# Norm, projection and dense attention put into one block each, the softmax maxima turned in f32 into four strips, and one division per unit

## The reference

```
h = layernorm(x) * (1 + ca) + sa
x = x + ga * L0_attn(h)        # 16 heads of 8, elu + 1 features, rotary, softmax over all 1024 keys, plus a 3-tap conv
x = x + gb * L0_ffn(h)         # two windowed-attention layers
x = x + ga * L1_attn(h)        # 16 heads of 8, softmax over all 1024 keys, then the mask of j >= i
x = x + gb * L1_ffn(h)         # four rounds of a four-expert mixture
```

## Time and profile before

| | |
|---|---|
| median of 3 runs | 1806.47 us (1805.66 to 1809.19) |
| the profiled execution | 1807.94 us |
| its span, first to last instruction | 1805.8 us |
| mean granted TensorE clock | 0.927 |
| busy share of the span | PE 87%, DVE 77%, ACT 66%, POOL 35% |
| first dense attention, first score to last value product | about 108 to 442 us |
| second dense attention, the same | about 1000 to 1350 us |

### The profile page before, as it was taken

How to read it: one execution, slowest core, us unless ns; L and a number is a source line. 1 busy time by engine, 2 the same in 40 slices (tenths; PEclk the granted TensorE clock), 3 DMA queues, 4 the chain that set the end, 5 groups by cost and what they waited for, 6 DMA issues and landing times. The chain is left out here.

```text
span 1805.8 us, 29185 instructions
## 1 busy us (share of the span) xinstructions
PE 1567.3 (87%) x11008; PEld 855.6 (47%) x11008; DVE 1385.4 (77%) x1948; ACT 1192.3 (66%) x2306; POOL 637.6 (35%) x516
## 2 busy tenths in 40 slices
PE   6589999997589887798986999999976699999998
PEld 4112222222356664566651233333324588788886
DVE  3899999993677546775437999999925399999996
ACT  2348888886367752677524677777772677877776
POOL 1930000000477551676204122222223255555554
PEclk9679999999689987899986899999996899999999
DMA  2320000000111100111003201111002011111111
GB/s 74 95 98 19 19 19 19 19 2 1 68 30 31 31 24 19 27 32 34 4 6 106 89 19 22 22 22 25 4 6 72 29 48 48 42 48 46 44 48 53
DMA packets 66875, 66.03 MB, mean 37 GB/s; under 512 B 39176, under 2 KB 42888, under 8 KB 66224
## 3 DMA queue, kind: packets, MB, share of 16 engines
q1 hardware_dynamic: 66096, 61.94, 11.9%
q10 hardware_dynamic: 576, 2.16, 0.3%
q0 software_dynamic: 64, 0.07, 0.0%
HBM read 40.85 MB, written 14.81 MB: 31 GB/s over the span
## 5 line engine op out<-in xcount | busy, mean ns | idle before, releaser
L878 ACT ACTIVATE att_probs<-psum 128x512 f32<-128x512 f32 x1024 | 535.2, 604 | 196.3 <-PE psum L806 195.7
L889 DVE TENSOR_REDUCE att_neg_max<-psum 128x1 f32<-128x1024 f32 x512 | 600.6, 1218 | 29.6 <-PE psum L777 23.8
L777 PE MATMUL psum<-att_k_op,att_q_op 48*128 48x512 bf16 x1024 | 350.4, 408 | 41.1 <-DMA att_k_op<-qk_parts 19.6
L806 PE MATMUL psum<-att_q_op,att_k_op 50*128 50x512 bf16 x1024 | 313.5, 387 | 19.6 <-ACT att_probs L878 19.6
L1973 ACT ACTIVATE moe_hidden<-psum,moe_b 128x512 f32<-128x512 f32 x256 | 167.4, 690 | 83.7 <-PE psum L76 83.5
L69 DVE TENSOR_TENSOR moe_hidden_low<-moe_hidden,moe_hidden_high 128x512 fp32r<-128x512 f32 x192 | 202.4, 1102 | 5.4 <-ACT moe_hidden_high L1979 5.3
L824 PE MATMUL psum<-att_probs,att_v 128*32 128x512 f32 (+2 forms) x1664 | 203.2, 558 | 2.9 <-ACT att_sums L870 2.8
L806 PEld LDWEIGHTS psum<-att_q_op,att_k_op 50*128 50x128 bf16 x1024 | 78.1, 94 | 251.1 <-ACT att_probs L878 187.7
L965 POOL TENSOR_TENSOR att_diag<-att_probs,att_triangle 128x512 f32<-128x512 f32 x64 | 82.0, 1280 | 272.7 <-PE psum L827 176.7
L2034 POOL TENSOR_TENSOR moe_hidden_low<-moe_hidden,moe_hidden_high 128x512 fp32r<-128x512 f32 x64 | 94.0, 1469 | 169.0 <-ACT moe_hidden_high L1979 168.9
L777 PEld LDWEIGHTS psum<-att_k_op,att_q_op 48*128 48x128 bf16 x1024 | 72.4, 95 | 165.5 <-DVE att_neg_max L889 120.4
(11 more groups left out here) (246 smaller groups left out, 2901.4 us busy)
## 6 DMA issues: line engine op xcount, KB each, us to landing
moe_spread_weights<-gate_rows SPq DMA_DIRECT2D x64, 256.0 KB, 3.2
wl_v_shift<-wl_v SPq DMA_DIRECT2D x62, 128.0 KB, 2.2
att_q_op<-qk_parts SPq DMA_DIRECT2D x32, 192.0 KB
att_k_op<-qk_parts SPq DMA_DIRECT2D x32, 192.0 KB
qk_parts<-att_hi SPq DMA_DIRECT2D x12, 256.0 KB, 4.2
qk_parts<-att_hi SPq DMA_DIRECT2D x12, 192.0 KB, 3.1
qk_parts<-att_mid SPq DMA_DIRECT2D x8, 256.0 KB, 4.3
moe_w<-in_moe_w SPq DMA_DIRECT2D x2, 1024.0 KB, 8.5
```

Source lines behind the costliest of these rows:

```text
L777: mm = pe.matmul(buf[:, half * CHUNK:(half + 1) * CHUNK], q_op[it % RING][at_rows(p, MAX_ROW), j, t * P:(t + 1) * P], k_op[it % RING][at_r ...
L806: pe.matmul(st_bank[e % 3], k_op[it % RING][at_rows(p, MAX_ROW + 2), j, t * P:(t + 1) * P], q_op[it % RING][at_rows(p, MAX_ROW + 2), j, ha ...
L878: act.activation(probs[:, g % PB, h, :], st_bank[e % 3], ACT.Exp, scale=scale).then_inc(exp_done, 1)
L889: dve.tensor_reduce(neg[:, t, p, j:j + 1], ring[e % 2], AX.X, ALU.max, negate=True).then_inc(ring_free, 1)
```

## The change

1. `layer_norm` and `project_heads` become a class `Projection`, whose steps are called inside the attention block. There is one block and no barrier between norm, projection and attention. The weights and tables are loaded at the block's start. The norm uses the existing per-chunk helper `ChunkNorm`. Its buffers and the projection's lie in the memory of the probabilities (`att_probs` in the names below).
2. The projection's steps have other lags: in the plain one hi, less_hi one step behind (before 3 and 4), mid and lo two behind (before 4). The value path uses one PSUM bank (7), the pair swap one bank (2).
3. The first 2 and the next 4 maxima stand in the last two steps of the projection (`EARLY`).
4. The maxima stay in f32 in a cleared tile of 16 columns a key tile; PE turns them by four f32 products with the identity, one for each strip of 32 partitions. DVE then takes hi of all 128 partitions (a copy) and subtracts it for the lower 64 (lo). SP sends the rows with four transfers (before two).
5. `turn` comes once per unit, one step later (g % 16 == 2), with eight transposes and one reciprocal and one product over all eight tiles.

```diff
+        self.LAST = NU + (4 if rotary else 2)
+
+    def at(self, t, lag):
+        return t - lag if 0 <= t - lag < self.STEPS else None
...
+    def norm_on_pe(self, pe):
+        for c in range(CHUNKS):
+            self.norm.average(pe, c)
+        for c in range(CHUNKS + 1):
+            if c < CHUNKS:
+                self.norm.variance(pe, c)
+            if c:
+                self.norm.spread_inverse(pe, c - 1)
+        pe.wait_ge(self.w_in, 16 * len(self.loads))
...
+    def step_on_pe(self, pe, t):
+        k, bank = self.k, self.bank
+        s = self.at(t, 0)
+        if s is not None:
+            if s % 2 == 0:
+                pe.wait_ge(self.norm.shifted, s // 2 + 1)
+            if s >= 2:
+                pe.wait_ge(self.drained if self.rotary else self.operand, s - 1)
+            pe.matmul(bank[s % 2], self.w[:, (s % 2) * DIM:(s % 2 + 1) * DIM], self.h[:, self.cols[s // 2]],
+                      start=True, stop=True).then_inc(self.projected, 1)
...
+            if s:
+                pe.wait_ge(self.swap_drained, s)
+            pe.matmul(bank[2], self.swap[:, :], self.val[:, s, :], start=True, stop=True).then_inc(self.swapped, 1)
+        if t % 2 == 1 and t // 2 < CHUNKS:
+            c = t // 2
+            if c:
+                pe.wait_ge(self.v_tok_done, c)
+            pe.matmul(bank[7], self.w[:, 2 * DIM:3 * DIM], self.h[:, self.cols[c]], start=True, stop=True)\
+                .then_inc(self.v_ps, 1)
...
+        s = self.at(t, 3 if self.rotary else 1)
+        if s is not None:
+            act.wait_ge(self.operand, s + 1)
+            act.activation(self.of(self.part[0], s), self.val[:, s, :], ACT.Copy).then_inc(self.hi_done, 1)
...
+        s = self.at(t, 4 if self.rotary else 1)
+        if s is not None:
+            dve.wait_ge(self.hi_done, s + 1)
+            dve.tensor_tensor(val[:, s, :], val[:, s, :], self.of(self.part[0], s), ALU.subtract)\
+               .then_inc(self.rest1, 1)
...
+        rec = sb("rec", [P, SEQ_TILES, GROUP])
...
+        proj = front(ctx, probs[:, :, :, :].rearrange("p a b n -> p (a b) n"))
...
-            if g % SEQ_TILES == 1 and g > SEQ_TILES:
-                out.append(("turn", g // SEQ_TILES - 1))
+            if g % STEPS == 2 and g > STEPS:
+                out.append(("turn", g // STEPS - 1))
...
+        EARLY = {proj.LAST - 2: first[0:2], proj.LAST - 1: first[2:6]}
...
                 it, half = n // 2, n % 2
                 sp.wait_ge(ring_free, number["rows", n] + 1)
                 for p in range(2):
-                    at = TILE_ROWS * p + MAX_ROW
-                    sp.dma_start(q_op[it % RING][at:at + 2, :, half * CHUNK:(half + 1) * CHUNK],
-                                 neg_rows[GROUP * p:GROUP * (p + 1), half * CHUNK:(half + 1) * CHUNK])\
-                      .then_inc(m_rows[half], 16)
+                    for j in range(2):
+                        at = TILE_ROWS * p + MAX_ROW
+                        sp.dma_start(q_op[it % RING][at:at + 2, j, half * CHUNK:(half + 1) * CHUNK],
+                                     neg_rows[2 * p + j::16, half, :])\
+                          .then_inc(m_rows[half], 16)
...
+            proj.load(sp)
+            operands.set_ones(sp)
+            proj.store_first(sp)
             for level in range(3):
                 operands.store(sp, 1, level)
             sp.wait_ge(operands.stored[1], 16 * 2 * TERMS)
...
             operands.load(sp, 2)
-            for level in range(3):
-                operands.store(sp, 2, level)
+            proj.store_second(sp)
...
             def rows(n):
                 buf = claim(("rows", n))
-                pe.wait_ge(hm_ready, n + 1)
-                for t in range(4):
-                    last = pe.matmul(buf[0:2 * GROUP, t * P:(t + 1) * P],
-                                     neg_parts[:, n % 2 * 4 + t, :, :, :].rearrange("p a c j -> p (a c j)"),
-                                     k.ident_bf[:, :], start=True, stop=True)
+                pe.wait_ge(neg_cleared, 1)
+                pe.wait_ge(ring_free, number["max", 2 * SEQ_TILES * (n + 1) - 1] + 1)
+                for strip in range(4):
+                    t = n % 2 * 4 + strip % 2 * 2
+                    last = pe.matmul(buf[32 * strip:32 * strip + 32, 0:P],
+                                     neg[:, t:t + 2, :].rearrange("p t r -> p (t r)"), k.ident[:, :],
+                                     start=True, stop=True)
                 last.then_inc(ring_ready, 1)
...
-                pe.wait_ge(evacuated, n + 1)
-                for t in range(4):
-                    last = pe.transpose(buf[:, t * P:(t + 1) * P], sums[:, n % 2, t * P:(t + 1) * P], k.ident[:, :])
+                pe.wait_ge(evacuated, 2 * n + 2)
+                for t in range(SEQ_TILES):
+                    last = pe.transpose(buf[:, t * P:(t + 1) * P], sums[:, t // 4, t % 4 * P:(t % 4 + 1) * P],
+                                        k.ident[:, :])
                 last.then_inc(ring_ready, 1)
...
+            proj.norm_on_pe(pe)
+            for t in range(proj.LAST):
+                proj.step_on_pe(pe, t)
+                lead(EARLY.get(t, ()))
+            lead(first[6:])
+            proj.scores_may_begin(pe)
...
+                    act.wait_ge(ring_ready, number["turn", n // 2 - 1] + 1)
...
+            proj.norm_on_act(act)
+            for t in range(proj.LAST):
+                proj.step_on_act(act, t)
+            proj.probabilities_may_begin(act)
...
                 dve.wait_ge(ring_ready, e + 1)
-                dve.tensor_reduce(neg[:, t, p, j:j + 1], ring[e % 2], AX.X, ALU.max, negate=True).then_inc(ring_free, 1)
-                if (m + 1) % (2 * SEQ_TILES) == 0:
-                    n = m // (2 * SEQ_TILES)
-                    at = slice(n % 2 * 4, n % 2 * 4 + 4)
-                    dve.wait_ge(ring_free, e + 1)
-                    dve.tensor_copy(neg_parts[:, at, :, 0, :], neg[:, at, :, :]).then_inc(hi_done, 1)
-                    dve.wait_ge(hi_done, n + 1)
-                    dve.tensor_tensor(neg_parts[:, at, :, 1, :], neg[:, at, :, :], neg_parts[:, at, :, 0, :], ALU.subtract)\
-                       .then_inc(hm_ready, 1)
+                dve.tensor_reduce(neg[:, t, 2 * p + j:2 * p + j + 1], ring[e % 2], AX.X, ALU.max, negate=True).then_inc(ring_free, 1)
...
             def rows(n):
                 e, it, half = number["rows", n], n // 2, n % 2
                 dve.wait_ge(ring_ready, e + 1)
                 if it:
-                    dve.wait_ge(m_rows[half], 32 * it)
-                dve.tensor_copy(neg_rows[:, half * CHUNK:(half + 1) * CHUNK], ring[e % 2][0:2 * GROUP, 0:CHUNK])\
+                    dve.wait_ge(m_rows[half], 64 * it)
+                dve.tensor_copy(neg_rows[:, half, :], ring[e % 2][:, 0:P]).then_inc(hi_done, 1)
+                dve.wait_ge(hi_done, n + 1)
+                low = neg_rows[64:P, half, :]
+                dve.tensor_tensor(low, ring[e % 2][64:P, 0:P], low, ALU.subtract)\
                    .then_inc(ring_free, 1)
...
-                if n + 1 == HALVES:
+                if n + 1 == UNITS:
                     dve.wait_ge(ring_free, e)
-                tile = ring[e % 2][:, 0:CHUNK].rearrange("p (t h c) -> p t h c", t=4, c=32)
+                tile = ring[e % 2].rearrange("p (t h c) -> p t h c", t=SEQ_TILES, c=32)
                 dve.reciprocal(rec[:, :, :], tile[:, :, :, HEAD_DIM]).then_inc(rec_done, 1)
                 dve.wait_ge(rec_done, n + 1)
-                out = k.att[:, 4 * half:4 * half + 4, it, :].rearrange("p t (h c) -> p t h c", c=HEAD_DIM)
+                out = k.att[:, :, n, :].rearrange("p t (h c) -> p t h c", c=HEAD_DIM)
                 num = tile[:, :, :, 0:HEAD_DIM]
-                by = rec[:, :, :].unsqueeze(3).broadcast_to([P, 4, GROUP, HEAD_DIM])
+                by = rec[:, :, :].unsqueeze(3).broadcast_to([P, SEQ_TILES, GROUP, HEAD_DIM])
                 dve.tensor_tensor(out, num, by, ALU.mult).then_inc(ring_free, 1)
...
+            proj.norm_on_dve(dve)
+            for t in range(proj.LAST):
+                proj.step_on_dve(dve, t)
+                if t == proj.LAST - 2:
+                    dve.wait_ge(neg_cleared, 1)
+                work(EARLY.get(t, ()))
+            work(order[6:])
...
+            pool.memset(neg[:, :, :], 0.0).then_inc(neg_cleared, 1)
+            operands.clear(pool)
...
-                with nc.sbuf_tensor("h0", [P, TOK], F32) as h:
-                    layer_norm(nc, k, "ln0", k.x, h, part(0, 1), part(0, 0))
-                    project_heads(nc, k, "rot", h, A, True, operands)
-                attention(nc, k, "att0", 1.0 / float(np.sqrt(HEAD_DIM)), False, operands, lepe.convolve)
+                h = ring.enter_context(nc.sbuf_tensor("h0", [P, TOK], F32))
+                norm_of = (k.x, part(0, 1), part(0, 0))
+                attention(nc, k, "att0", 1.0 / float(np.sqrt(HEAD_DIM)), False, operands,
```

(22 more changed lines are left out.)

381 lines of the change are left out of this document (180 added, 201 removed).

## The result

The changed kernel takes 1786.84 us (median of 4 runs, 1785.31 to 1789.51), the kernel before 1806.58: ratio 0.989, 95% interval 0.9873 to 0.9907. Forecast was 1778, range 1768 to 1791. The profiled execution took 1787.71 us, 20.2 us less than that of before, where the sum said 28.4; its span is 1785.9, 19.9 less.

The account below looks back on a forecast made before the run. DVE was taken to set each half of the attention loop, with PE almost full. First head 10.0, second head 7.6, loops 5.6 and 5.2 sum to 28.4 us off 1807.94: 1779.5, as a median 1778, range 1768 to 1791.

Parts of the forecast that it names:

- The bound and the rows in the loop: Attention loops: DVE sets the half; PE's wait behind the rows goes, saving 5.6 us in first attention, 5.2 in causal.
- Division per unit: Attention loops: one division per unit saves DVE 0.4 us a half but doesn't shorten the half; PE and ACT set it.
- strips on PE: Rows in the loop: four f32 products replace four bf16 ones on PE, 0.42 us against 0.39, costing nothing.
- Four transfers: Rows in the loop: four transfers replace two; the fourth lands 0.35 us before it is needed, so costed at nothing.
- Split ahead of the first score: First head: the held SBUF split goes, 4.1 us of stall and 0.3 for small operations, less 1.0 for `less_hi`.
- That `less_hi`: First head: the last `less_hi` now stands between maxima 2 and 3 on DVE, costing 1.0 us, 1.4 at worst.
- Seam of the first head: First attention, norm to projection: without the barrier DVE's first projection operation begins at 31.0, not 37.63, gaining 6.6 us.
- I take this shift as kept through the projection: First head: the 6.6 us carries to last store, load and first maximum, since DVE's and POOL's operations set the projection's period.
- Rival B: The heads give less: single-bank value path and swap make engines wait, or the subtraction is held; 1784 us, chance 0.11.
- Second head: Second attention's norm and projection: 4.9 us from the seam, 2.4 from shorter lags, 0.3 from the split; sum 7.6.
- I take 2.4: Second projection: shorter lags leave ACT 20 operations for 24, cutting 3.0 us from 17.9, taken as 2.4.

Follow-up runs that it names:

- second series: The changed kernel run again word for word, nothing changed: 1782.91 us, ratio 0.9861.
- loops alone: The kernel before with only the loop's part of the change (f32 maxima in four strips, four transfers, division once a unit), heads as before: 1789.65 us, ratio 0.9904.
- heads alone: The changed kernel with the loop's part undone (split in SBUF, one copy, two transfers, division per half), new heads kept: 1794.5 us, ratio 0.9933.
- first series: The changed kernel's own first measurement, against the kernel before: 1786.84 us, ratio 0.989.
- held stores: The changed kernel with SyncE waiting for the first unit's operands before it stores the other groups' parts: 1785.4 us, ratio 0.9871.
- PE filled: The changed kernel with one more f32 product of 384 columns in PE's idle time in the norms before both projections: 1783.41 us, ratio 0.9874.
- two value banks: The changed kernel with the transposed values in a PSUM bank of their own: 1784.18 us, ratio 0.9878.
- five mends: The changed kernel with own value bank, two swap banks, held stores, PE filled in the norm, no maxima ahead of the last `less_hi`: 1775.85 us, ratio 0.9836.

## Why the prediction was right, and where its sizes were off

**The bound and the rows in the loop: right.** The half is 20.46 us (predicted 20.4), the wait behind the rows went from 0.39 to 0.17 (I had said that none would be left), and the loops gave 10.55 us for 10.8 (11.3 in the second series). That the sum came so close is luck, since two misses cancel. First attention 3.8 for 5.6: the two steps behind the rows went from 2.89 + 2.47 to 2.54 + 2.52, 0.3 us a half and not 0.4. Causal 6.75 for 5.2: in the seven halves where VectorE is the limit the three steps around the rows went from 3.20 + 3.18 + 2.64 to 2.83 + 2.64 + 2.64, 0.9 us and not 0.55, and in the others only 0.05 went, for 0.2.

**Division per unit and strips on PE at nothing: right.** Undone, the division costs 1 to 1.8 us in the loops, and 0.03 a unit in their middle; the strips take PE 0.40 us. I called VectorE's time for the new rows 0.6; it is 0.28 + 0.29.

**Four transfers at nothing: right**, with 0.7 us of slack. The landing from the issue's start, which I put at 1.7 from a 64 KB row, was 1.62. The room was 4.08 and not 3.96, an issue took 0.60 and not 0.63, and each of the four moves 2 KB, not the 4 KB that I wrote.

**Split ahead of the first score: right in sum.** From first maximum to first score 27.18 us for 31.03: 3.85, forecast 3.4. The new subtraction wasn't held (0.29 beside GpSimd's 5.45), as the Trainium skill, "SBUF — State Buffer", "Who interferes with whom", says of an operation with at most one input in SBUF. In the loops alone, where no `less_hi` stands between the maxima, the stretch takes 26.67: 4.36 for the 4.4 that I had for stall and small operations. That `less_hi` costs 0.5 us and not 1.0 (27.18 for 26.64 and 26.66 in the two kernels with no maxima ahead of it). But these 4 us were a meeting of two operations and no property of the code: in the heads alone 2.3 of them had gone without touching the split.

**Seam of the first head: the step that failed is "I take this shift as kept through the projection".** VectorE's first operation comes 3.3 us earlier in one execution and 6.6 in the other (31.00, as predicted), by PE's clock in the norm. Then the projection is longer. From there to the last store it takes 31.46 us and 32.94, for 30.58. In both, VectorE's cosine product waits for GpSimd and is then held beside it, 1.74 us for 0.68. In both, PE's second swap product waits 1.96 us for the single swap bank. The difference is PE's clock behind that wait. It stays at 1.00 in the first series and is 0.50 in the second (40.5 to 43.5), and there VectorE waits 1.79 us for the next projection product. First series, then second:

```profile
42.91 1.10 PE L545 MATMUL psum<-att_probs,rot_swap 128*128 128x512 f32 x2 [1.96 <-DVE att_probs L609]
```
```profile
44.14 0.75 DVE L596 TENSOR_SCALAR att_probs<-psum,rot_b 128x512 f32<-128x512 f32 x1 [1.79 <-PE psum L536]
```

The four kernels with one bank that take 32.9 to 33.0 us are the four with this fall of the clock; with two banks it came in none of four. That speaks for the wait at the bank as what lets it fall, and four are few. Rival B's single swap bank so has a part in the loss, 1.5 us where the clock fell. The load takes 0.6 to 0.7 more; that the other groups' stores in the same DMA engines do this, which the old barrier had kept away, is borne out by the held stores. So 6.6 became 1.8 and 3.5 at the first maximum.

**Second head: the step that failed is "I take 2.4" for the shorter lags.** From the norm's first product to ACT's first bias it is 16.85 us for 22.33, 5.5 (forecast 4.9). With like clocks it is 14.94 in the second series for 19.55 with the loops alone: 4.6. From there to the last store 18.75 and 17.73 us, for 17.92: in these two executions the lags gave nothing (-0.8 and 0.2). I counted ACT's operations, and ACT isn't full there. `v_tok` is first in its step, and waits for VectorE's three operations on the same chunk of values and for PE's transposes (1.42, then 1.11 for the product queued behind). I had named the wait in rival B, but by the wrong cause, the one bank: with a second bank it stays.

PE waits too, ahead of these transposes, and the sum had no term for what that does to its clock. The changed kernel, first series:

```profile
935.04 0.85 PE L556 MATMUL psum<-ident,v_ch 128*128 128x128 f32 x4 [2.54 <-DVE v_ch L623]
935.69 1.91 PE L536 MATMUL psum<-h,plain_w 128*128 128x512 f32 x2
```

The kernel with PE filled in the norm, at the same place:

```profile
932.61 0.66 PE L561 MATMUL psum<-ident,v_ch 128*128 128x128 f32 x4 [2.53 <-DVE v_ch L628]
933.11 1.02 PE L541 MATMUL psum<-h,plain_w 128*128 128x512 f32 x2
...
933.31 0.60 ACT L571 ACTIVATE v_tok<-psum 128x512 f32<-128x512 f32 x1 [1.26 <-PE psum L561]
934.17 0.69 ACT L579 ACTIVATE att_probs<-psum,plain_b 128x512 f32<-128x512 f32 x1 [0.26 <-PE psum L541]
```

After the same wait the clock is 0.50 in the first (935.5 to 938.7, and again 942.4 to 945.4) and 1.00 in the second, through the whole stretch. At 0.50 the next product takes 1.91 us for 1.02, and ACT waits 1.11 for it and not 0.26. The twelve profiled kernels with the new heads sort by the number of such falls: none, 15.92 us (PE filled); one, 17.60 to 17.94 (seven kernels), and 16.51 in one; two, 18.74 to 18.78 (the changed kernel, two value banks, five mends). So at the full clock the lags gave up to 2.0 us of the 2.4, in one kernel (before, the first 2.6 us of the stretch ran at 0.50). The falls took that back. The filling product stands in the norm, and two of the three kernels with it had falls here, so what decides them isn't shown. That ACT's and PE's waits come from the shorter lag is read from the trace; a kernel with the old lag alone wasn't run. Behind that, the last store to the load costs 1.3 to 1.6 more, the load 1.0 to 1.4.

What stays open is why the last store lands later. The changed kernel, in both series, and five others with one value bank show 3.5 to 4.0 us, the four with two banks 2.21, but so do the heads alone, with one.

**And 1.4 us are luck.** In the experts' norm VectorE's first long operation was held 4.13 us beside GpSimd before, and 2.80 now; no edit is near it.

## What to carry over

When a barrier goes, look at what it had kept apart: transfers that now share the DMA engines with the load on the path, and operations of VectorE and GpSimd that now meet. A shorter software lag counts in full only where the engine is full; with a round trip over three engines in front of an in-order queue, the lag was the cover. Read PE's granted clock behind each of its waits as well: here a wait of 0.8 to 2.5 us between f32 products often cost a second time, by products at half the clock. And a kernel of this length has stretches that move by up to 5 us without being touched, so cut two traces at the same marks before giving a difference to an edit.

## What the runs showed that I had not expected

- PE's granted clock behind an idle time of 0.82 us in the norm was at 2.4 GHz in some executions of one kernel and at 1.2 GHz in others (1.00 and 0.54 from 27 to 32), worth 3.3 us at VectorE's first projection operation. In the second norm it fell in eleven kernels of eleven, and with a product in the idle time in none of three.
- The second projection took 15.92, 17.60 to 17.94 or 18.74 to 18.78 us by how often the clock fell in it, with one exception (16.51).
- The same small VectorE operation on SBUF took 0.17 us with no GpSimd operation beside it, and 1.46 or 4.27 beside one, by what was left of that one.
- The windowed stretch, 480 us of unchanged code, took 478.84 to 484.19 us.
